# FFN layer one as three products of rounded parts, and the first loads in one queue

## The reference, cut to what matters

```python
x = layernorm(x + attn(x))      # x: 4 x 2048 x 256
x = layernorm(x + ffn(x))

# attn: layer norm with gamma and beta, Q, K, V and gate from 256 to 1024 (16 heads of 64),
#       h = alpha * h + k v^T, o = q h, o * silu(gate), 1024 back to 256

def ffn(x):
    gf = global_net(x.mean(axis=1, keepdims=True))      # 256 -> 128 -> 64 -> 1
    out = x
    for _ in range(3):
        tf = coupling_net(out)                          # layer one: gelu(out @ w1 + b1), 256 -> 256
        combined = 0.7 * gf + 0.3 * tf
        coupling = 0.1 + adaptive_range * (combined - 0.5) * 2.0
        out = out + coupling * twist(out)
    return out
# twist: the four quarters (o_r, o_i, p_r, p_i) become (p_r, -p_i, -o_r, o_i)
```

## Time and profile before

| | before |
|---|---|
| median of 3 runs | 1774.66 us |
| the profiled execution, its own time | 1774.2 us |
| its span | 1772.5 us |
| TensorE (PE) busy | 1700.9 us, 96% |
| VectorE (DVE) busy | 1125.7 us, 64% |
| ScalarE (ACT) busy | 735.3 us, 41% |
| GpSimd (POOL) busy | 458.6 us, 26% |
| mean granted clock of TensorE | 0.992 |

### The profile page before, as it was taken

The page is one execution under the profiler, slowest core; times in us unless marked ns, Lnnn a source line. Parts: engine busy times, 40 slices in busy tenths (PEclk is TensorE's granted clock), DMA queues, the critical chain, the costliest instruction groups (busy, mean ns, idle before and its releaser), DMA issues.

```text
span 1772.5 us, 50035 instructions
## 1 busy us (share of the span) xinstructions
PE 1700.9 (96%) x21776; PEld 1318.5 (74%) x21776; DVE 1125.7 (64%) x2580; ACT 735.3 (41%) x1387; POOL 458.6 (26%) x464
## 2 busy tenths in 40 slices
PE   4999999999999999999999999999999999999992
PEld 3888888874688888885578888888468888888641
DVE  5667676755476767674466767676456676766553
ACT  3334242444443434343634343434445343434445
POOL 5323232310232323231022323232013232323101
PEclk9999999999999999999999999999999999999996
DMA  4000000000000000000000000000000000000001
GB/s 159 14 2 14 2 14 2 14 1 1 1 26 2 26 3 25 6 22 1 1 14 14 14 14 14 14 14 14 1 1 14 13 14 14 14 13 3 13 1 48
DMA packets 23098, 26.49 MB, mean 15 GB/s; under 512 B 3424, under 2 KB 21728, under 8 KB 22880
## 3 DMA queue, kind: packets, MB, share of 16 engines
q1 hardware_dynamic: 21152, 20.14, 3.5%
q10 hardware_dynamic: 1728, 3.15, 0.5%
HBM read 14.90 MB, written 8.39 MB: 13 GB/s over the span
## 4 chain that ended last, share of the span: by engine, by line
PE 86%; DVE 6%; ACT 4%; issue 2%; POOL 1%; DMA 0%; ACTq 0%; DVEq 0%; SPq 0%; POOLq 0%
PE bank L1140 39%; PE bank L1220 11%; PE bank L1167 7%; PE bank L1207 6%; PE bank L1385 6%; PE bank L1184 4%; PE bank L1197 4%; PE bank L1416 3%; PE bank L1176 3%; PE bank L1124 2%; PE bank L1438 1%; ACT q_sb L607 1%; DVE att L909 1%; DVE v_sb L967 1%; DVE q_sb L865 1%
## 5 line engine op out<-in xcount | busy, mean ns | idle before, releaser
L488 POOL TENSOR_TENSOR k_end<-k_sc,pows 128x512 f32<-128x512 f32 x128 | 135.0, 1055 | 635.7 <-DVE k_sc L856 634.3
L607 ACT ACTIVATE q_sb<-q_sb,pows 128x384 f32<-128x384 f32 (+2 forms) x384 | 167.6, 499 | 242.5 <-DVE q_sb L865 242.5
L1017 DVE SCALAR_TENSOR_TENSOR h_seq<-h_seq,pows,bank 128x64 f32<-128x64 f32 x384 | 107.8, 281 | 247.1 <-PE bank L1184 236.5
L623 ACT ACTIVATE h_sc<-h_seq,pows 128x256 f32<-128x256 f32 x128 | 65.3, 510 | 429.4 <-DVE h_seq L1017 429.4
L497 POOL TENSOR_TENSOR o_lo<-o_g,o_hi 128x512 fp32r<-128x512 f32 x128 | 165.2, 1291 | 144.0 <-ACT o_hi L629 141.1
L909 DVE COPY_PREDICATED att<-causal,bank 128x1024 f32<-128x1024 int32 x128 | 168.0, 1313 | 0.5
L1220 PE MATMUL bank<-wo_hi,o_hi 128*128 128x256 f32 x512 | 149.1, 291 | 1.8 <-POOL o_lo L497 1.8
L629 ACT ACTIVATE o_hi<-o_g 128x512 fp32r<-128x512 f32 x128 | 80.8, 631 | 154.2 <-DVE o_g L925 154.2
L1220 PE MATMUL bank<-wo_hi,o_lo 128*128 128x256 f32 x512 | 144.4, 282 | 0.0
L1220 PE MATMUL bank<-wo_lo,o_hi 128*128 128x256 f32 x512 | 144.1, 281 | 0.0
L1207 PE MATMUL bank<-att,v_sb 128*64 128x128 f32 x2048 | 140.1, 279 | 0.6 <-DVE att L909 0.6
(11 more groups left out here) (197 smaller groups left out, 3762.4 us busy)
## 6 DMA issues: line engine op xcount, KB each, us to landing
x_in<-in_x SPq DMA_DIRECT2D x16, 512.0 KB, 3.9
out_y<-x1t SPq DMA_DIRECT2D x32, 256.0 KB, 2.3
v_sb<-in_wq ACTq DMA_DIRECT2D x1, 1024.0 KB, 6.3
x1t<-in_wv ACTq DMA_DIRECT2D x1, 1024.0 KB, 8.9
q_sb<-in_wo ACTq DMA_DIRECT2D x1, 1024.0 KB, 16.1
v_sb<-in_wk SPq DMA_DIRECT2D x1, 1024.0 KB, 11.4
x1t<-in_wg SPq DMA_DIRECT2D x1, 1024.0 KB, 13.9
bias_v<-in_bV SPq DMA_DIRECT2D x1, 512.0 KB, 14.3
```

The source lines that it names most:

```text
L488: nc.gpsimd.tensor_tensor(k_end[:].rearrange("p (a z) (b r) -> p a (z b) r", z=2, r=BL), k_sc[:].rearrange("p (a z) (b r) -> p a (z b) r", ...
L607: last = nc.scalar.activation(q_sb[:, p % 2, d].rearrange("p (a z) n -> p a (z n)", z=2)[:, :, reach], q_sb[:, p % 2, 0].rearrange("p (a z ...
L1017: step = nc.vector.scalar_tensor_tensor(h_seq[:, c + 1, :] if c + 1 < NC else h_st[:, p, :], h_seq[:, c, :], pows[:, p, HP + 1:HP + 2], ba ...
```

## The change

1. `f_w1` is replaced by `w1_hi` and `w1_lo` (float32r). w1 is loaded into a part of `z_x`; VectorE makes a rounded copy, subtracts it, and writes the twisted half of both (four TENSOR_SCALAR operations where there were two). TensorE's wait for this setup is raised to 19.
2. `rows_made` calls `products` with x1 in rounded parts: six float32r matmuls for a product where there were two of float32. The parts are made in portions `u` of 256 tokens, eight a batch. ScalarE writes the high part to `o_hi` (`x1_part_high`), GpSimd the low part to `o_lo` (`x1_part_low`); portions take the two places of those tiles in turn. A portion of u > 1 waits until the two products of portion u - 2 are done, portions 0 and 1 wait for the last two `y_part`s of the step.
3. The order: ScalarE makes portion 0 between the queries' shift and the gate of the next batch's first pair, portion 1 behind that pair, portions 2 to 5 behind every second `rows_kept`, portions 6 and 7 behind the two `layer1`s of the first visit. GpSimd has portions 0 and 1 ahead of the fourth step's `pow`, the others behind it.
4. Start: all weights go through SP's queue, in the order x, wq, five constants, wk, wv, bias_v, wg, other constants, wo. ScalarE takes wk's high part behind the first x, VectorE the low part of x ahead of that of wk.
5. Storage: `z_first` becomes a part of `h_st`, so `states_cleared` moves behind the last coupling of a batch; `mix` shrinks from 9 to 6 tables, with two more waits in `mix_ended`; `vare2` shares `rstd2`; alpha's tables lie in `z_x`.

```diff
-        f_w1 = sb("f_w1", [P, KT, 2 * D])
+        w1_hi = sb("w1_hi", [P, KT, 2 * D], f32r)
+        w1_lo = sb("w1_lo", [P, KT, 2 * D], f32r)
...
             sp.dma_start(x_in[:], x_rows[0]).then_inc(s_x, 16)
+            load_weight(sp, 0)
             for dst, src in first_consts:
                 sp.dma_start(dst, src).then_inc(s_first, 16)
             load_weight(sp, 1)
+            load_weight(sp, 2)
+            for dst, src in consts[:1]:
+                sp.dma_start(dst, src).then_inc(s_const, 16)
             load_weight(sp, 3)
-            for dst, src in consts:
+            for dst, src in consts[1:]:
                 sp.dma_start(dst, src).then_inc(s_const, 16)
+            sp.dma_start(wo_in, a["wo"].rearrange("(n p) m -> p n m", p=P)).then_inc(s_wo, 16)
...
+            def x1_part_low(b, u):
+                pool.wait_ge(s_xrh, b * NS * 2 + u + 1)
+                nc.gpsimd.tensor_tensor(halved(o_lo, u), x1_part(u), halved(o_hi, u).bitcast(f32),
+                                        ALU.subtract).then_inc(s_xrl, 1)
...
+            def x1_part_high(b, u):
+                if u > 1:
+                    act.wait_ge(s_z, b * NS * NC + 2 * u - 2)
+                else:
+                    act.wait_ge(s_yp, (b + 1) * NS * NP - 1 + u + C0)
+                if u == NS * 2 - 2:
+                    act.wait_ge(s_x1c, (b + 1) * NS * KT + C0)
+                nc.scalar.activation(halved(o_hi, u), x1_part(u), ACT.Copy).then_inc(s_xrh, 1)
...
                 for t in range(GT):
-                    for c in range(NC):
-                        rows_kept(b, t, c)
+                    for half in range(2):
+                        rows_kept(b, t, 2 * half)
+                        rows_kept(b, t, 2 * half + 1)
+                        x1_part_high(b, 2 * t + half + 2)
...
             weight_low(0, "q")
+            low_part(0)
             weight_low(1, "k")
-            low_part(0)
...
-            for k in range(KT):
-                nc.vector.tensor_scalar(f_w1[:, k, D:2 * D], f_w1[:, 1 - k, 0:D], sign[:, 1 - k:2 - k], None,
-                                        ALU.mult).then_inc(s_setv, 1)
+            nc.vector.tensor_copy(w1_hi[:, :, 0:D], w1_in).then_inc(s_setv, 1)
+            dve.wait_ge(s_setv, 9)
+            nc.vector.tensor_tensor(w1_lo[:, :, 0:D], w1_in, w1_hi[:, :, 0:D].bitcast(f32), ALU.subtract).then_inc(s_setv, 1)
+            dve.wait_ge(s_setv, 10)
+            for tile in (w1_hi, w1_lo):
+                for k in range(KT):
+                    nc.vector.tensor_scalar(tile[:, k, D:2 * D], tile[:, 1 - k, 0:D].bitcast(f32), sign[:, 1 - k:2 - k], None,
+                                            ALU.mult).then_inc(s_setv, 1)
...
-                    if t == NS - 1 and c == 0:
-                        pe.wait_ge(s_x1c, (b + 1) * NS * KT + C0)
-                    for k in range(KT):
-                        last = nc.tensor.matmul(z_bank(t, c), x1t[:, k, t * ST + c * C:t * ST + (c + 1) * C],
-                                                f_w1[:, k, :], start=(k == 0), stop=(k == KT - 1))
-                    last.then_inc(s_z, 1)
+                    unit = 2 * t + c // 2
+                    tok = slice(c % 2 * C, (c % 2 + 1) * C)
+                    pe.wait_ge(s_xrl, b * NS * 2 + unit + 1)
+                    products(z_bank(t, c), 0, 6,
+                             lambda k: halved(o_hi, unit)[:, k, tok], lambda k: halved(o_lo, unit)[:, k, tok],
+                             lambda k: w1_hi[:, k, :], lambda k: w1_lo[:, k, :]).then_inc(s_z, 1)
```

More of the change, by code:

```diff
@@ L115, in build @@
         two = sb("two", [P, NC, GT])
-        mix = sb("mix", [P, NG, 9, NC, GT])
+        mix = sb("mix", [P, NG, 6, NC, GT])
         mv2 = sb("mv2", [P, NS, NC, 2])
-        vare2 = sb("vare2", [P, NS, NC])
         rstd2 = sb("rstd2", [P, NS, NC])
@@ L308, in build @@
             (bias_o[:], a["bO"].unsqueeze(0).broadcast_to([P, D])),
-            (f_w1[:, :, 0:D], a["cn_w1"].rearrange("(k p) n -> p k n", p=P)),
+            (w1_in, a["cn_w1"].rearrange("(k p) n -> p k n", p=P)),
             (f_w2[:], a["cn_w2"].rearrange("(k p) n -> p k n", p=P)),
@@ L386, in turns_done, with x1_part, halved @@
             return b * VIS * GT + v * GT + j + 1
+        def x1_part(u):
+            t, half = u // 2, u % 2
+            return x1t[:, :, t * ST + half * D:t * ST + (half + 1) * D]
+        def halved(tile, u):
+            return tile[:, u % 2, :].rearrange("p (k n) -> p k n", k=KT)
         def zm_done(b, g, i, j):
@@ L558, in _ @@
                     o_low(NP - 1, (it + 1) * NP - 1)
+                    if s == NS - 1:
+                        x1_part_low(b, 0)
+                        x1_part_low(b, 1)
                     pool.wait_ge(s_r1, it + 1)
                     nc.gpsimd.tensor_tensor(rstd[:], vare[:], half_neg[:], ALU.pow).then_inc(s_rs1, 1)
+                for u in range(2, 2 * NS):
+                    x1_part_low(b, u)
                 mix_begun(b, 0)
```

49 lines of the change are left out of this document (27 added, 22 removed).

## The result

The changed kernel takes 1750.14 us (median of 4 runs, 1748.44 to 1752.71), the kernel before 1774.85 beside it; the ratio is 0.9863 (95% interval 0.9851 to 0.9874). The execution that was profiled is the slowest of the four, 1752.71 us (span 1751.0); its mean granted clock is 0.989, that of the other three 0.990 to 0.992.

A forecast was written before the change was run, and what follows sets the result against it. TensorE, with 86% of the chain of waits, was taken as the bound. 1774.2 - 20.2 (layer one) + 2.0 (bubbles) - 1.4 (start) = 1754.6, stated as 1755.0 us because the median lay 0.46 higher; range 1751.5 to 1760.0.

The forecast's parts named there:

- Layer one on TensorE: Layer one's 64 products fall from 1.716 to 1.40 us each, 20.2 us less, all on the path.
- What feeds it: Making layer one's high and low parts leaves TensorE bubbles of 0.5 us a batch, 2.0 us in all (bounds 0.4 to 7).
- GpSimd would wait behind VectorE's norm operations: Portion 2's low part in layer one: up to 0.35 us a batch; as a rival in every batch, 1760, chance 0.08.
- the sum over x1: Second eight products of layer one: this sum starts 0.63 us later behind portion 5's copy; 0.2 us put down.
- Clearing the state: Moved behind the last coupling, where VectorE idles: costs nothing; without that cover, 0.48 us in three batches.
- the waits in the mix: Two added waits lie a whole layer visit ahead of the next use: cost nothing.
- The start: Chain to the first kept value: earlier x gains 3.65 us, VectorE's added setup costs 2.25, net 1.4 us gained.
- The clock in the start: Rival: TensorE idles 4.3 us before the first kept value, the clock falls, costing 1.5 to 3 us; chance 0.25.
- a late x: Rival: in the start x lands as late as before and setup is paid in full, 1758.6 us; chance 0.1.
- a change without effect: Rival: copying rows, not TensorE, sets layer one's stretch; result near 1774 us; chance 0.02.
- exposed weight loads: Rival: each layer-one matmul's own weight load shows, up to 2.38 us a product, 1815 us; chance 0.03.

The follow-up runs named there:

- x_parts: Changed kernel with TensorE reading x_hi and x_lo in layer one without waiting for the portions, which are still made; 1751.04 us.
- start_only: Kernel before with only the change's new start (order of loads, wk's parts behind x), without layer one's change or its setup; 1770.99 us, ratio 0.9979.
- after_back64: Changed kernel with two 32-byte tiles moved behind x1t, so the big tiles stand 64 bytes further back; 1755.89 us, ratio 0.9889.
- w1_at0: Changed kernel with the 32-byte tile rng3 moved ahead of w1_hi, so w1_hi and w1_lo start on a multiple of 128 bytes; 1749.72 us.
- before_pad64: Kernel before with 64 unused bytes a partition ahead of its big tiles, moving x, o and the rest but not the attention's weights; 1771.58 us, ratio 0.9981.
- before_all64: Kernel before with 64 unused bytes a partition ahead of all its tiles, so weights, x and o all move; 1773.99 us, ratio 1.0001.
- setup_late: Changed kernel with the six VectorE operations on w1 moved from the start into the first attention step; 1747.6 us, ratio 0.9849.

## Why the prediction was wrong, point by point

Faster was right, and so was the mechanism of its largest term. The sum, 19.6 us gained, fell 5.1 short of the measured 24.7. The step that failed is the one that put the change of storage at nothing and gave the attention steps no term: they became 3.75 us shorter. Beside it, one cost was put too high.

- **Layer one on TensorE**: right. 0.316 us a product was forecast; 0.234 a matmul gives 1.40, the copies of rows 1.42, against 1.716. The rows of the values' matmuls decided rightly against the longer duration and against the 215.7 ns that the Trainium skill, page "TensorE: Matmul & The Clock Gate", section "Wait — 56ns, not 53.3ns?", gives: no mean of 128x512 in these traces came below 226.
- **What feeds it**: mis-sized. 0.5 us a batch were put down, `x_parts` shows 0.1, and the one late portion in the trace of after (0.25 and 0.31 in place of twice 0.234) comes to about 0.1. Layer one gained 4.89 us a batch in the first three, 4.56 were forecast (64 x 0.316 less 2.0, over four). What was wrong here is that GpSimd would wait behind VectorE's norm operations, and that the sum over x1 would delay TensorE: the first two did collide, and VectorE paid, while the second left no wait. The Trainium skill, page "GPSIMD Engine Reference", section "1. Specifications", says that GpSimd contends with VectorE's instructions in a two-port mode or with two SBUF inputs. This trace shows contention, 2.44 for 1.38 us, on VectorE, which nobody waited for here; it does not show the mode of VectorE's operations.
- **Clearing the state**, the waits in the mix, the sum over x1: nothing, as put.
- **The start**: the two terms were nearly exact and so was their difference. The path came 3.75 us earlier by `start_only` (3.65 forecast), the setup cost 2.17 (2.25 forecast): 1.58 net against 1.4. In part that is luck: x itself came only 3.33 us earlier in this trace, and the old start varies (6.02 and 7.55 us for x).
- **The clock in the start**: a rival with a chance of 0.25, and it happened. TensorE idled 3.46 us (4.3 was forecast), and the fall cost 1.3 us, just under the 1.5 to 3 of the rival: six matmuls at half pace, not eight. All four traces with a wait of 3.46 or 3.47 us there (after, `after_back64`, `w1_at0`, `x_parts`) show the fall, and none with 1.69 or less. Waits between the two were not tried. It is put right by taking the setup off the path.
- **What was missing**: the prediction took from the storage part of the change only the cleared state and the two waits in the mix, "nothing" both times, and the sum has no term for the attention steps, which the diff does not touch. But the new w1 tiles and the tables taken out left every tile of x and o 64 bytes past a multiple of 128, with the weights on one, and 15 steps became a quarter of a microsecond shorter, 3.75 us. `before_pad64` and `after_back64` show it alone, in both directions. No bound of the prediction held it, and without it the time would have been near 1754. The size of the effect could not be read from any row of before.
- **Added up**: 19.6 (four times 4.89) + 3.75 + 1.6 - 1.3 = 23.6 us, of the 24.7 by the medians; 0.65 of the difference is that the profiled execution of before is faster than its median, the rest lies within the spread. The last batch's fall of the clock is in some traces and not in others and costs 1.6 to 1.8 us: in the profiled execution of after it leaves 21.9. Measured there were 21.5; behind TensorE's last matmul this execution takes 0.4 longer than that of before (33.05 and 32.62).

The rivals of a late x, of a change without effect and of exposed weight loads did not happen: no matmul of layer one cost more than the spacing of the earlier trace rows once the clock was up.

## What to carry to other kernels

When a diff adds or removes a tile, work out by how many bytes the tiles behind it move, and compare the spacing of matmuls that the diff does not touch: in this kernel moving one side by 64 bytes was worth 3.6 or 9 us. Price a matmul by start-to-start times from a stretch with its own form, and ask of each contention which of the two engines is the one waited for. Before setup work is put in front of TensorE's first long wait, see whether a later step can hide it; here the wait cost its length and then 1.3 us by the pace of what followed.

## What the runs showed of the hardware that I had not expected

- The spacing of float32r matmuls depends on where the stationary and the moving tile stand to each other in SBUF: with the same tiles, data and order of instructions the values' are 228.9 to 233.2 ns apart, the gate's 228.9 to 234.7, y_part's (128x256) 118.9 to 122.6. Moving both by 64 bytes changes nothing (232.4 and 232.5, 232.9 and 232.7, 122.2 and 122.2). In layer one the placements tried differ by 1.2 ns at most (233.1 to 234.3).
- GpSimd's subtraction of 128x512 took 1.29 us beside VectorE's norm operations as without them, and those took 2.44 us in place of 1.38; the first of them lasted until the subtraction had ended.
- The granted clock of after fell at 33.15 us, 2.9 us after TensorE's last work before the gap; in the other three traces with a wait of 3.46 or 3.47 us it fell 2.4 to 4.0 us after, in two of them when the work had begun again. In the last batch it fell in 4 of the 13 traces that have the wait of 1.8 us there (after, `before_pad64`, `before_all64`, `setup_late`), so a wait of that length is no safe one.
